# Second attention of a two-stage kernel: one ScalarE copy moved within its round, and the last batch's last four heads added by VectorE

## The chip, the cores and the metric

The kernel runs on one core of a Trainium2 chip. The metric is device time in microseconds of that core, as the median of several executions. A profiled execution gives instruction times of the core's engines: TensorE (PE; its weight loads are shown apart as PEld), VectorE (DVE), ScalarE (ACT), GpSimd (POOL) and SyncE (SP), which here only starts DMAs.

## The reference, cut to what matters

Two stages over x of shape (8, 512, 512). The first stage is a gated cross-attention whose result, x1, goes to DRAM; the change doesn't touch it. The second stage is this, for each of the 8 batches:

```python
# x: layernorm of x1; h = 8 heads, dh = 64, e = 5 experts, SEL = 2
q = (x @ Wq).reshape(b, t, h, dh).transpose(0, 2, 1, 3)
k = (x @ Wk).reshape(b, t, h, dh).transpose(0, 2, 1, 3)
gl_v = (x @ Ws).reshape(b, t, h, e)
wv = _topk_mask(gl_v, SEL) * jax.nn.sigmoid(gl_v)
xv = jnp.einsum('btd,edk->btek', x, Wv)
v = jnp.einsum('bthe,btek->bhtk', wv, xv)
scores = jnp.einsum('bhid,bhjd->bhij', q * scale, k)
probs = jax.nn.softmax(scores, axis=-1)
attn = jnp.einsum('bhij,bhjd->bihd', probs, v)
gl_o = (x @ Wd).reshape(b, t, h, e)
mask_o = _topk_mask(gl_o, SEL)
out = jnp.einsum('bthe,bthk,ekd->btd', mask_o, attn, Wo)
# result: x1 + tanh(g_ffn) * out
```

## The kernel before, in words

**Tiling.** A batch has 512 rows, which are 4 row tiles (t = 0 to 3) of 128. The 8 heads are taken in 4 pairs. Each head has 4 row tiles of scores, so a batch has 32 tiles of 128x512 scores (STEPS). Products of fp32 accuracy are made of three fp32r matmuls, of a high part, which ScalarE copies out of PSUM, and a low part, which VectorE forms as the difference.

**Rounds.** The order of the work is written out by hand. A round is four tiles of scores: it has the places SCORES, BEFORE, TURNS, BEHIND and AFTER, in this order on each engine. In SCORES, TensorE multiplies the scores, VectorE takes row maxima (L1496) and ScalarE the exponentials (L1370). In TURNS, TensorE transposes the four tiles of probabilities (L1791), and ScalarE copies the transposed tiles to SBUF as `pt` (probs_copy, L1379). The other units of work (`AT`) have a round and a place: turn_y is the transposition of the normalised x1, experts is the product with the stacked expert and gate weights (L1743), q and k are their products (L1734), values is probabilities times values (L1804), turn_o the transposition of a pair's output (L1749), turn_z and result the transposition of z and the product with Wo (L1757, L1767). Scores occupy rounds 0 to 7 of a batch; its units run from round -3 to round 12. So the steady loop (`Fori(0, B - 1)`, 7 passes) runs rounds 5 to 12 of batch b together with rounds -3 to 4 of batch b + 1. Rounds 5 to 12 of the last batch follow by themselves.

**Three shared banks.** All of these units but values write to one of three PSUM banks of `ps_r`, in turn, in the order `ORDER` of the steady loop. TensorE waits, before a unit, until the unit that is three places earlier in `ORDER` has been read (wait_bank, wait_read). In round 6 of batch b, which is round -2 of batch b + 1, the order on the banks is: experts 0, turn_y 2, turn_y 3 (place BEFORE), then experts 1, experts 2 (place BEHIND), then turn_o 1 (AFTER). So experts 1 uses the bank of experts 0 and waits for both of its copies, which are ScalarE's: `logits` (L1405) and `xv` (L1408). The copies of experts 0 begin with a wait for `v_steps`, GpSimd's count of steps, which says that the values of all pairs of the batch before are mixed and that `xv` may be overwritten.

```python
elif name == "experts":
    act.wait_ge(ex_ps, b * NT + n + 1)
    if n == 0 and not first:

        act.wait_ge(v_steps, b * PAIRS * V_STEPS)
        act.wait_ge(mask_ready, b)
```

**The mix over experts.** GpSimd mixes the values of each pair (mix_values: multiplications L1313, additions L1319). The output of the attention goes to z, 128 rows x 320 (5 experts x 64) per row tile, which is the sum over heads of (normalised output of the head) x (coefficient of row, head and expert). For each head h, VectorE makes a product over all four row tiles and experts, 128x1280 (mix_product, L1510; head 0 writes z, the others `z_tmp`, two buffers in turn). GpSimd adds heads 1 to 5 to z (mix_sums, L1331), and VectorE heads 6 and 7 (mix_sum, L1521). The products of pair p stand in rounds 5, 7, 9 and 10, and the coefficients in rounds 3, 5, 7 and 8 (L1534). Then ScalarE copies the last 64 columns of z once more (copy_last, L1423), z is transposed in three column tiles, ScalarE and VectorE split it (L1418, L1558), the four results are multiplied out, VectorE adds each to the residual (L1565), and SyncE stores it.

Of the kernel before, what the change touches and what calls it, by code (L numbers as in the profile page):

```python
# [20 lines left out]
F32 = mybir.dt.float32  # L21
# [3 lines left out]
ALU = mybir.AluOpType  # L25
# [3 lines left out]
P = 128  # L29
# [986 lines left out]
def expert_attention(nc, block, both, x1, g_ffn, wk, wo, out):  # L1016
# [3 lines left out]
    B, T, D = x1.shape  # L1020
# [58 lines left out]


    CUT = 5
    assert all(CUT - ROUNDS <= n < CUT + ROUNDS for n, place in AT.values())

    def units_at(n, *places):

        return [what for what, at in AT.items() if at[0] == n and at[1] in places]
# [9 lines left out]
    def bank_of(what):  # L1096
        return ORDER.index(what) % RING

    with ExitStack() as mem:
# [3 lines left out]
        def sem(name):  # L1103
            return mem.enter_context(nc.semaphore(name + "_2"))
# [83 lines left out]
        z_pool = sem("z_pool")  # L1188
        z_copied = sem("z_copied")
        z_ready = sem("z_ready")  # L1190
        zt_ps = sem("zt_ps")
# [98 lines left out]
        def _(pool):  # L1290
# [50 lines left out]
            with pool.Fori(0, B - 1) as b:  # L1341
                mix_sums(b, LAST_PAIR - 1)
                mix_values(b + 1, 0)
                rest(b + 1)
            mix_sums(B - 1, LAST_PAIR - 1)

        @block.scalar
        def _(act):
# [76 lines left out]
            def step(b, n, place, first=False):  # L1425
# [9 lines left out]
                elif place == BEFORE:  # L1435
                    if n == COPY_LAST_AT:
                        copy_last(b)
                    units_hi(b, units_at(n, BEFORE), first)
                    if n == 0:

                        act.wait_ge(logits_ready, b * NT + NT)
                        act.activation(sig[:], logits[:, 0], ACT.Exp, scale=-1.0).then_inc(sig_exp, 1)
                elif place == TURNS:
                    if 0 <= n < ROUNDS:
                        for tile in range(n * BANKS, n * BANKS + BANKS):
                            probs_copy(b, tile, first)
                elif place == BEHIND:
                    if n == NORMALISE_AT and not first:
                        normalise(b, (2, 3))
                    units_hi(b, units_at(n, BEHIND, AFTER), first)  # L1450

# [15 lines left out]
            with act.Fori(0, B - 1) as b:  # L1467
                for n in range(CUT, CUT + ROUNDS):
                    for place in PLACES:
                        step(b, n, place)  # L1470
                        step(b + 1, n - ROUNDS, place)
            for n in range(CUT, CUT + ROUNDS):
                for place in PLACES:
                    step(B - 1, n, place)

        @block.vector
        def _(dve):
# [170 lines left out]
            def units_lo(b, units, first):  # L1648
                for name, i in units:
                    if name != "values" and not (first and name == "turn_y"):  # L1650
                        part_lo(b, name, i)

            dve.wait_ge(both.feat_ps, B * NT)

# [10 lines left out]
            with dve.Fori(0, B - 1) as b:  # L1665
                for n in range(CUT, CUT + ROUNDS):
                    for place in PLACES:
                        step(b, n, place)
                        step(b + 1, n - ROUNDS, place)
            for n in range(CUT, CUT + ROUNDS):  # L1670
                for place in PLACES:
                    step(B - 1, n, place)

        @block.tensor
        def _(pe):
# [37 lines left out]
            def shared(b, name, n, first, last):  # L1713
# [45 lines left out]
                else:  # L1759
                    if n == 0:  # L1760
                        pe.wait_ge(w_lo["wo"], KZ)
                        pe.wait_ge(cleared, 2)
                    every = [(k, l, r) for k in range(LAST) for l, r in PASSES] + [(LAST, 1, 0), (LAST, 1, 1)]
                    for m, (k, l, r) in enumerate(every):
                        if n == 0 and m % len(PASSES) == 0:
                            pe.wait_ge(zt_lo, b * KZ + k + 1)
                        end = pe.matmul(ps, z_t2[:, l, k, n * P:(n + 1) * P], wo2[:, r, k, :],  # L1767
                                        start=m == 0, stop=m == len(every) - 1)
                    end.then_inc(res_ps, 1)

# [24 lines left out]
            def values(b, p, first):  # L1795
# [10 lines left out]
                end.then_inc(o_ps, 1)  # L1806

            def step(b, n, place, first=False, last=False):

# [13 lines left out]
            with pe.Fori(0, B - 1) as b:  # L1823
                for n in range(CUT, CUT + ROUNDS):
                    for place in PLACES:
                        step(b, n, place)
                        step(b + 1, n - ROUNDS, place)
            for n in range(CUT, CUT + ROUNDS):
                for place in PLACES:
                    step(B - 1, n, place, last=True)  # L1830


# [65 lines left out]
```

## Time and profile before

| | |
|---|---|
| Median of 3 runs | 1232.3 us (1231.46 to 1234.57) |
| Profiled execution, its own time | 1232.12 us |
| Its span in the profile | 1230.3 us |
| TensorE busy | 1187.6 us, 97% of the span |
| VectorE busy | 832.2 us, 68% |
| GpSimd busy | 662.3 us, 54% |
| ScalarE busy | 642.5 us, 52% |

The span is the time from the first to the last record of the profile; the time of the execution has 1.8 us more around it. Times in the rows are microseconds from the start of the span. One pass of the steady loop takes 86.6 us.

### The profile page before, as it was taken

The numbers are of one execution on the slowest core, as the hardware profiler recorded it, in microseconds if no ns is written. First come the engines' busy times: TensorE is split into PE (matmuls) and PEld (weight loads), VectorE is DVE, ScalarE is ACT, GpSimd is POOL, SyncE is SP. The second block draws the span as 40 slices with busy tenths as digits, with TensorE's granted clock in tenths as the row PEclk, the third lists the DMA queues.
The fourth block names the chain that finished last, engine by engine and source line by source line (L and its number), as shares of the span: only waits on it lengthen the run. The fifth ranks groups of instructions, "written<-read, shape, count | busy, mean of one in ns | idle before, by whom it ended". The sixth has DMA issues, their size and how long they took to land.

```text
span 1230.3 us, 19712 instructions
## 1 busy us (share of the span) xinstructions
PE 1187.6 (97%) x6344; PEld 912.0 (74%) x6344; DVE 832.2 (68%) x1526; ACT 642.5 (52%) x1431; POOL 662.3 (54%) x481
## 2 busy tenths in 40 slices
PE   5899999999999999999999999999999999999995
PEld 4678888888888887875767767777777777777663
DVE  6777777777777766367575674766765765756765
ACT  5443434334343433467566666566656666666661
POOL 1724242424242425339379297397496494692893
PEclk9899999999999999999999999999999999999998
DMA  6341414141414122410002002002011011020010
GB/s 206 119 129 43 128 43 128 43 128 43 128 43 128 43 94 99 153 50 1 35 2 90 13 0 102 0 20 83 0 43 59 0 68 34 0 68 0 0 69 35
DMA packets 40746, 75.87 MB, mean 62 GB/s; under 512 B 3728, under 2 KB 4240, under 8 KB 40720
## 3 DMA queue, kind: packets, MB, share of 16 engines
q1 hardware_dynamic: 40720, 75.55, 18.4%
q8 instruction: 13, 0.21, 0.1%
q14 instruction: 13, 0.11, 0.0%
HBM read 58.76 MB, written 16.78 MB: 61 GB/s over the span
## 4 chain that ended last, share of the span: by engine, by line
PE 66%; POOL 22%; DVE 5%; issue 5%; ACT 1%; POOLq 1%; DMA 0%; SPq 0%; DVEq 0%
PE ps_f L878 20%; POOL spare L1319 10%; POOL spare L1313 10%; PE ps_r L1734 8%; PE ps_h L878 8%; PE ps_s L878 7%; PE ps_r L1743 5%; PE ps_s L1791 4%; PE ps_s L1783 4%; PE ps_o L1804 4%; PE ps_r L1767 2%; PE ps_t L912 1%; DVE nmax L1496 1%; DVE z_tmp L1510 1%; POOL z L1331 1%
## 5 line engine op out<-in xcount | busy, mean ns | idle before, releaser
L1370 ACT ACTIVATE tmp<-ps_s,nmax 128x512 f32<-128x512 f32 x256 | 172.7, 688 | 106.8 <-DVE nmax L1496 106.8
L1496 DVE TENSOR_REDUCE nmax<-ps_s 128x1 f32<-128x512 f32 x256 | 158.7, 682 | 100.0 <-PE ps_s L1783 99.7
L1331 POOL TENSOR_TENSOR z<-z,z_tmp 128x1280 f32<-128x1280 f32 x40 | 117.1, 2928 | 178.8 <-DVE z_tmp L1510 176.1
L1313 POOL TENSOR_TENSOR spare<-xv,pick 128x512 f32<-128x512 f32 x160 | 168.1, 1051 | 34.8 <-DVE pick L1605 21.7
L1319 POOL TENSOR_TENSOR spare<-spare 128x512 f32<-128x512 f32 x128 | 180.5, 1410 | 10.0
L1379 ACT ACTIVATE pt<-ps_s 128x512 f32<-128x512 f32 x256 | 132.6, 621 | 10.8 <-PE ps_s L1791 10.8
L1791 PE MATMUL ps_s<-ident,tmp 128*128 128x128 f32 x1024 | 125.0, 273 | 2.6 <-ACT tmp L1370 2.5
L1791 PEld LDWEIGHTS ps_s<-ident,tmp 128*128 128x128 f32 x1024 | 114.9, 140 | 13.4 <-ACT tmp L1370 6.9
L1804 PE MATMUL ps_o<-pt,spare 128*64 128x512 f32 x512 | 116.9, 598 | 0.0
L255 POOL TENSOR_TENSOR e_t<-e_t 128x512 fp32r<-128x512 f32 x32 | 40.7, 1296 | 141.5 <-ACT e_t L474 141.5
L1783 PE MATMUL ps_s<-k,q 64*128 64x512 f32 x768 | 107.0, 409 | 2.2 <-DVE k L1552 1.5
L1783 PEld LDWEIGHTS ps_s<-k,q 64*128 64x128 f32 x768 | 67.4, 184 | 46.1 <-issue 34.0
L255 POOL TENSOR_TENSOR c<-stage,c 128x512 fp32r<-128x512 f32 x28 | 42.4, 1544 | 105.7 <-ACT c L251 105.7
L878 PE MATMUL ps_s<-c_t,es_t 128*128 128x512 f32 x384 | 96.2, 403 | 2.9 <-DVE es_t L255 2.9
L878 PE MATMUL ps_h<-es_t,c 128*128 128x512 f32 x384 | 98.8, 407 | 0.0
L1734 PE MATMUL ps_r<-es_t,wk 128*128 128x512 f32 x384 | 97.1, 401 | 0.0
L1734 PE MATMUL ps_r<-es_t,c_t 128*128 128x512 f32 x384 | 96.6, 400 | 0.0
L878 PE MATMUL ps_f<-weh,eh_t 128*128 128x512 f32 x384 | 94.7, 396 | 0.0
L878 PE MATMUL ps_f<-wh,h_t 128*128 128x512 f32 x384 | 93.5, 393 | 0.0
L878 PE MATMUL ps_f<-wec,e_t 128*128 128x512 f32 x384 | 92.3, 393 | 0.4 <-DVE wec L255 0.4
L878 PEld LDWEIGHTS ps_s<-c_t,es_t 128*128 128x128 f32 x384 | 72.4, 192 | 19.2 <-DVE es_t L255 4.1
L1734 PEld LDWEIGHTS ps_r<-es_t,wk 128*128 128x128 f32 x384 | 70.3, 188 | 21.0 <-issue 5.8
(183 smaller groups left out, 2100.1 us busy)
## 6 DMA issues: line engine op xcount, KB each, us to landing
stage<-in_x SPq DMA_DIRECT2D x32, 256.0 KB, 3.1
x_sb<-in_x SPq DMA_DIRECT2D x8, 1024.0 KB, 5.3
x_dram<-x_sb SPq DMA_DIRECT2D x32, 256.0 KB, 2.6
stage<-x_dram SPq DMA_DIRECT2D x8, 1024.0 KB, 5.7
x_sb<-x_dram SPq DMA_DIRECT2D x8, 1024.0 KB, 5.7
out_dram<-x_sb SPq DMA_DIRECT2D x32, 256.0 KB, 2.0
stage<-in_ctx_t SPq DMA_DIRECT2D x28, 256.0 KB, 2.8
stage<-in_ctx SPq DMA_DIRECT2D x28, 256.0 KB, 2.7
```

The costliest lines, as they stand in the source:

```text
L255: return eng.tensor_tensor(pair[:, 1, k, :], operand[:, k, :], pair[:, 0, k, :].bitcast(F32), ALU.subtract)
L878: last = pe.matmul(out, left(l, k), right(r, k), start=start and n == 1, stop=stop and n == ND * len(PASSES))
L1313: pool.tensor_tensor(v_tmp[:] if e else acc, xv[:, :, e, :].unsqueeze(2).broadcast_to(shape), pick[:, 0, e, :, 2 * p:2 * p + 2].unsqueeze( ...
L1319: pool.tensor_tensor(acc, acc, v_tmp[:], ALU.add).then_inc(v_steps, 1)
L1331: pool.tensor_tensor(zv, zv, z_tmp[:, h % 2], ALU.add).then_inc(z_pool, 1)
L1370: act.activation(probs[:, n % BANKS, :], ps_s[:, n % BANKS, :], ACT.Exp, bias=nmax[:, n:n + 1], accum_out=den[:, h, t:t + 1]).then_inc(p_e ...
L1379: act.activation(pt[:, h % 4, :, t * P:(t + 1) * P], ps_s[:, n % BANKS, :].rearrange("p (k t) -> p k t", k=NT), ACT.Copy).then_inc(pt_read ...
L1496: dve.tensor_reduce(nmax[:, n:n + 1], ps_s[:, n % BANKS, :], AX_X, ALU.max, negate=True).then_inc(nmax_ready, 1)
L1734: end = pe.matmul(ps, w2[:, l, k, n * P:(n + 1) * P], y_t2[:, r, k, :], start=m == 0, stop=m == len(every) - 1)
L1783: end = pe.matmul(ps_s[:, (n + a) % BANKS, :], q2[head_rows(a), p % 2, l, t * P:(t + 1) * P], k2[head_rows(a), p % 2, r, :], start=m == 0, ...
L1791: end = pe.transpose(ps_s[:, n % BANKS, k * P:(k + 1) * P], probs[:, n % BANKS, k * P:(k + 1) * P], ident[:])
L1804: end = pe.matmul(ps_o[head_rows(a), :], v_acc[:, p, k, a, :], pt[:, p % 2 * 2 + a, k, :], start=k == 0, stop=k == NT - 1)
```

## The change: what it does

First, the name LATE. The two ScalarE copies of the unit experts 0 leave the place BEFORE of round -2, where they stood ahead of the copies of turn_y 2 and turn_y 3 and ahead of the four copies of probabilities, and go to the place BEHIND of the same round, behind these six copies and ahead of the copies of experts 1. TensorE's order and its waits stay as they are. This concerns all 7 passes of the steady loop, and the prologue, where no probabilities are copied in that round.

Second, the last batch's end. Rounds 5 to 9 of it stay for TensorE and ScalarE, 5 to 8 for VectorE. GpSimd no longer adds heads 4 and 5 of the last batch. Heads 4 to 7 are added to z by VectorE, with one instruction for each head, row tile and expert (add_head): z's 128x64 share becomes coefficient x (128x64 of PSUM) + share. For heads 4 and 5 all four row tiles are done; for heads 6 and 7 and what follows, row tile by row tile: after the two heads of tile t its last 64 columns are copied again (copy_share), TensorE transposes the tile's three column tiles into one bank, ScalarE copies them in two pieces, VectorE forms the low part of the tile before (end_lo) and adds the result of the tile before that (end_out). TensorE makes 24 transpositions of the identity, whose output is not used, after turn_o 3.

```diff
--- before.py
+++ after.py
@@ -1078,6 +1078,12 @@
     COPY_LAST_AT = 11
+    LATE = ("experts", 0)
+    END_AT = 9
     CUT = 5
     assert all(CUT - ROUNDS <= n < CUT + ROUNDS for n, place in AT.values())
@@ -1095,6 +1101,8 @@
     def bank_of(what):
         return ORDER.index(what) % RING
+    END_BANKS = [bank for bank in range(RING) if bank != bank_of(("turn_o", PAIRS - 1))]
     with ExitStack() as mem:
         def sb(name, shape, dt=F32):
@@ -1187,6 +1195,7 @@
         z_dve = sem("z_dve")
         z_pool = sem("z_pool")
         z_copied = sem("z_copied")
+        z_heads = sem("z_heads")
         z_ready = sem("z_ready")
         zt_ps = sem("zt_ps")
         zt_hi = sem("zt_hi")
@@ -1342,7 +1351,6 @@
                 mix_sums(b, LAST_PAIR - 1)
                 mix_values(b + 1, 0)
                 rest(b + 1)
-            mix_sums(B - 1, LAST_PAIR - 1)
         @block.scalar
         def _(act):
@@ -1435,7 +1443,7 @@
                 elif place == BEFORE:
                     if n == COPY_LAST_AT:
                         copy_last(b)
-                    units_hi(b, units_at(n, BEFORE), first)
+                    units_hi(b, [what for what in units_at(n, BEFORE) if what != LATE], first)
                     if n == 0:
                         act.wait_ge(logits_ready, b * NT + NT)
@@ -1447,6 +1455,8 @@
                 elif place == BEHIND:
                     if n == NORMALISE_AT and not first:
                         normalise(b, (2, 3))
+                    if n == AT[LATE][0]:
+                        units_hi(b, [LATE], first)
                     units_hi(b, units_at(n, BEHIND, AFTER), first)
             def units_hi(b, units, first):
@@ -1469,9 +1479,15 @@
                     for place in PLACES:
                         step(b, n, place)
                         step(b + 1, n - ROUNDS, place)
-            for n in range(CUT, CUT + ROUNDS):
+            for n in range(CUT, END_AT + 1):
                 for place in PLACES:
                     step(B - 1, n, place)
+            out_copy(B - 1, LAST_PAIR, False)
+            for t in range(NT):
+                act.wait_ge(zt_ps, (B - 1) * KZ + t + 1)
+                turned = ps_r[:, END_BANKS[t % 2], 0:KZ * P].rearrange("p (k t) -> p k t", k=KZ)
+                act.activation(z_t2[:, 0, 0:LAST, t * P:(t + 1) * P], turned[:, 0:LAST, :], ACT.Copy)
+                act.activation(z_t2[:, 1, LAST, t * P:(t + 1) * P], turned[:, LAST, :], ACT.Copy).then_inc(zt_hi, 1)
         @block.vector
         def _(dve):
@@ -1650,6 +1666,58 @@
                     if name != "values" and not (first and name == "turn_y"):
                         part_lo(b, name, i)
+            def add_head(h, t, end=False):
+                ps = ps_r[:, bank_of(("turn_o", h // 2)), :].rearrange("p (t a k) -> p t a k", t=NT, a=2)[:, t, h % 2, :]
+                for e in range(E):
+                    share = z[:, t, e * DH:(e + 1) * DH]
+                    last = dve.scalar_tensor_tensor(share, ps, coef[:, h, t, e:e + 1], share, ALU.mult, ALU.add)
+                return last
+            def copy_share(t):
+                dve.tensor_scalar(z_all[:, t, NV:KZ * P], z[:, t, NV - HALF:NV], 1.0, None, ALU.mult).then_inc(z_ready, 1)
+            def end():
+                b = B - 1
+                first_sums = b * POOL_SUMS + 2 * LAST_PAIR - 3
+                dve.wait_ge(z_pool, first_sums)
+                dve.wait_ge(to_ps, b * PAIRS + LAST_PAIR)
+                for h in (2 * LAST_PAIR - 2, 2 * LAST_PAIR - 1):
+                    if h % 2:
+                        dve.wait_ge(z_heads, 1)
+                    for t in range(NT):
+                        last = add_head(h, t)
+                    last.then_inc(z_heads, 1)
+                dve.wait_ge(to_ps, b * PAIRS + PAIRS)
+                for t in range(NT + 2):
+                    if t < NT:
+                        dve.wait_ge(z_heads, 2 + 2 * t)
+                        add_head(2 * LAST_PAIR, t).then_inc(z_heads, 1)
+                        dve.wait_ge(z_heads, 3 + 2 * t)
+                        add_head(H - 1, t).then_inc(z_heads, 1)
+                        dve.wait_ge(z_heads, 4 + 2 * t)
+                        copy_share(t)
+                    if 1 <= t <= NT:
+                        end_lo(b, t - 1)
+                    if t >= 2:
+                        end_out(b, t - 2)
+            def end_lo(b, t):
+                cols = slice(t * P, (t + 1) * P)
+                turned = ps_r[:, END_BANKS[t % 2], 0:KZ * P].rearrange("p (k t) -> p k t", k=KZ)
+                dve.wait_ge(zt_hi, b * KZ + t + 1)
+                dve.tensor_tensor(z_t2[:, 1, 0:LAST, cols], turned[:, 0:LAST, :], z_t2[:, 0, 0:LAST, cols].bitcast(F32),
+                                  ALU.subtract)
+                dve.tensor_tensor(z_t2[HALF:P, 1, LAST, cols], turned[HALF:P, LAST, :],
+                                  z_t2[HALF:P, 1, LAST, cols].bitcast(F32), ALU.subtract).then_inc(zt_lo, 1)
+            def end_out(b, t):
+                if t == 0:
+                    dve.wait_ge(xres_loaded, b * 16 + 16)
+                dve.wait_ge(res_ps, b * NT + t + 1)
+                dve.scalar_tensor_tensor(x_res[:, t, :], ps_s[:, t, :], gate[:, 0:1], x_res[:, t, :],
+                                         ALU.mult, ALU.add).then_inc(out_ready, 1)
             dve.wait_ge(both.feat_ps, B * NT)
             dve.memset(norm[:], 0.0).then_inc(out_ready, NT)
@@ -1667,9 +1735,10 @@
                     for place in PLACES:
                         step(b, n, place)
                         step(b + 1, n - ROUNDS, place)
-            for n in range(CUT, CUT + ROUNDS):
+            for n in range(CUT, END_AT):
                 for place in PLACES:
                     step(B - 1, n, place)
+            end()
         @block.tensor
         def _(pe):
@@ -1760,13 +1829,16 @@
                     if n == 0:
                         pe.wait_ge(w_lo["wo"], KZ)
                         pe.wait_ge(cleared, 2)
-                    every = [(k, l, r) for k in range(LAST) for l, r in PASSES] + [(LAST, 1, 0), (LAST, 1, 1)]
-                    for m, (k, l, r) in enumerate(every):
-                        if n == 0 and m % len(PASSES) == 0:
-                            pe.wait_ge(zt_lo, b * KZ + k + 1)
-                        end = pe.matmul(ps, z_t2[:, l, k, n * P:(n + 1) * P], wo2[:, r, k, :],
-                                        start=m == 0, stop=m == len(every) - 1)
-                    end.then_inc(res_ps, 1)
+                    result(ps, n, (lambda k: pe.wait_ge(zt_lo, b * KZ + k + 1)) if n == 0 else None)
+            def result(ps, t, ready=None):
+                every = [(k, l, r) for k in range(LAST) for l, r in PASSES] + [(LAST, 1, 0), (LAST, 1, 1)]
+                for m, (k, l, r) in enumerate(every):
+                    if ready and m % len(PASSES) == 0:
+                        ready(k)
+                    last = pe.matmul(ps, z_t2[:, l, k, t * P:(t + 1) * P], wo2[:, r, k, :], start=m == 0,
+                                     stop=m == len(every) - 1)
+                last.then_inc(res_ps, 1)
             def scores(b, n, first):
@@ -1804,6 +1876,24 @@
                         end = pe.matmul(ps_o[head_rows(a), :], v_acc[:, p, k, a, :], pt[:, p % 2 * 2 + a, k, :],
                                         start=k == 0, stop=k == NT - 1)
                 end.then_inc(o_ps, 1)
+            def end(b):
+                shared(b, "turn_o", LAST_PAIR, False, True)
+                for _ in range(24):
+                    pe.transpose(ps_s[:, NT - 1, 0:P], ident[:], ident[:])
+                for t in range(NT + 1):
+                    if t < NT:
+                        pe.wait_ge(z_ready, b * 2 + t + 1)
+                        if t >= 2:
+                            pe.wait_ge(zt_lo, b * KZ + t - 1)
+                        for k in range(KZ):
+                            last = pe.transpose(ps_r[:, END_BANKS[t % 2], k * P:(k + 1) * P],
+                                                z_all[:, t, k * P:(k + 1) * P], ident[:])
+                        last.then_inc(zt_ps, 1)
+                    if t:
+                        pe.wait_ge(zt_lo, b * KZ + t)
+                        result(ps_s[:, t - 1, :], t - 1)
             def step(b, n, place, first=False, last=False):
@@ -1825,9 +1915,10 @@
                     for place in PLACES:
                         step(b, n, place)
                         step(b + 1, n - ROUNDS, place)
-            for n in range(CUT, CUT + ROUNDS):
+            for n in range(CUT, END_AT + 1):
                 for place in PLACES:
                     step(B - 1, n, place, last=True)
+            end(B - 1)
 def program(nc, x, ctx, ctx_t, g_xattn, g_ffn, w_sim, w_sim_cols, b_sim, w_qv, b_qv, wq, wk, w_vsd, wo, x1, out):
```

## Rows read from the trace of the kernel before

**Rows 1.** Page: busy time, share, instructions of each engine; slices of the granted clock.

```profile
PE 1187.6 (97%) x6344; PEld 912.0 (74%) x6344; DVE 832.2 (68%) x1526; ACT 642.5 (52%) x1431; POOL 662.3 (54%) x481
...
PEclk9899999999999999999999999999999999999998
```

**Rows 2.** Waits of TensorE, whole span: total, times, longest, in us.

```profile
PE ps_r L1757 <- DVE z L1521: 7.8, 1, 7.8
...
PE ps_r L1743 <- ACT logits L1405: 4.6, 8, 1.5
```

**Rows 3.** All waits from 540 to 1210 us, the same columns.

```profile
ACT logits L1405 <- POOL spare L1319: 13.4, 7, 2.0
```

**Rows 4.** Timeline, last steady pass, round 6: start, us, engine, line, operation, idle before.

```profile
1105.18 1.03 PE L1725 MATMUL ps_r<-ident,stage 128*128 128x128 f32 x8
...
1105.61 0.21 ACT L1370 ACTIVATION_READ_ACCUMULATOR tmp<-ps_s,nmax 128x1 f32 x1
...
1106.05 1.91 PE L1791 MATMUL ps_s<-ident,tmp 128*128 128x128 f32 x16
...
1106.41 1.27 POOL L1319 TENSOR_TENSOR spare<-spare 128x512 f32<-128x512 f32 x1
...
1107.71 0.24 ACT L1405 ACTIVATE logits<-ps_r 128x80 f32<-128x80 f32 x1 [1.89 <-POOL spare L1319]
1107.84 0.43 ACT L1408 ACTIVATE xv<-ps_r 128x320 f32<-128x320 f32 x1
...
1108.16 1.10 ACT L1397 ACTIVATE es_t<-ps_r 128x512 fp32r<-128x512 f32 x2
...
1108.37 4.57 PE L1743 MATMUL ps_r<-c,es_t 128*128 128x400 f32 x24 [0.41 <-ACT logits L1405]
...
1109.12 2.10 ACT L1379 ACTIVATE pt<-ps_s 128x512 f32<-128x512 f32 x4
```

**Rows 5.** Timeline, the last batch's end.

```profile
1197.67 5.88 POOL L1331 TENSOR_TENSOR z<-z,z_tmp 128x1280 f32<-128x1280 f32 x2 [0.35 <-DVE z_tmp L1510]
...
1203.53 2.88 DVE L1510 TENSOR_TENSOR z_tmp<-ps_r,coef 128x1280 f32<-128x1280 f32 x2
...
1205.09 5.92 POOL L1331 TENSOR_TENSOR z<-z,z_tmp 128x1280 f32<-128x1280 f32 x2 [1.54 <-DVE z_tmp L1510]
...
1207.22 0.63 PE L1749 MATMUL ps_r<-ident,spare 128*128 128x128 f32 x4 [0.79 <-ACT spare L1387]
...
1212.45 3.08 DVE L1521 TENSOR_TENSOR z<-z,z_tmp 128x1280 f32<-128x1280 f32 x2
...
1218.26 8.81 PE L1767 MATMUL ps_r<-wo,z_t 128*128 128x512 f32 x32
...
1227.11 0.75 DVE L1565 SCALAR_TENSOR_TENSOR x_sb<-ps_r,gate,x_sb 128x512 f32<-128x512 f32 x1 [1.10 <-PE ps_r L1767]
```

**Rows 6.** Timeline of VectorE, first stage.

```profile
130.27 0.23 DVE L645 TENSOR_SCALAR ew<-ew,bsim_col 128x4 f32<-128x4 f32 x1
130.41 1.00 DVE L631 TENSOR_SCALAR tmp<-e_t,w_cols 128x512 f32<-128x512 f32 x2
...
133.39 0.75 DVE L814 SCALAR_TENSOR_TENSOR x_sb<-ps_f,gate,x_sb 128x512 f32<-128x512 f32 x1
134.06 0.54 DVE L631 TENSOR_SCALAR tmp<-e_t,w_cols 128x512 f32<-128x512 f32 x1
```

**Rows 7.** Groups by line and form: busy us, mean ns of one, idle before.

```profile
L1548 DVE SCALAR_TENSOR_TENSOR q<-ps_r,q 128x512 fp32r<-128x512 f32 x32 | 21.8, 682 | 20.3 <-ACT q L1412 20.3
```

**Rows 8.** Busy time by stretch (engines in turn), granted clock (PEclk), DMA share, GB/s.

```profile
32.60:36.70 4.10, 0.66 (x4) 0.42 (x4) 2.83 (x14) 3.75 (x9) 1.24 (x2) 0.96 0.72 254
...
514.00:517.60 3.60, 2.10 (x12) 1.78 (x11) 1.46 (x3) 2.64 (x6) 2.55 (x3) 1.00 0.42 159
1210.52:1215.60 5.08, 0.00 (x0) 0.00 (x0) 4.38 (x3) 0.04 (x1) 0.48 (x1) 0.50 0.00 0
1215.60:1220.70 5.10, 5.03 (x18) 4.41 (x19) 2.08 (x3) 2.17 (x4) 0.00 (x0) 0.50 0.01 3
```


## The prediction

> **What bounds the kernel now.** I read the page first: TensorE is busy for 97% of the span, at the full clock (2.4 GHz) in nearly every slice [rows 1]. So an edit pays only if it removes TensorE work, which this one doesn't, or a wait of TensorE, and it costs wherever it adds one. Then the waits of TensorE: in the second attention only two matter. One is short and comes again: the product with the experts (L1743) waits for ScalarE's copies of experts 0, 8 times, 4.6 us in all, of which 1.5 us is in the first one. The other comes once: the transposition of z at the end of the last batch waits 7.8 us for VectorE [rows 2]. Then the stretch around each, in the timeline. Both parts of the change lie at one of these two waits.
>
> **The copies of experts 0, before.** In the last steady pass ScalarE is done with the exponentials of round 6 at 1105.61 + 0.21 = 1105.82. It then stands for 1.89 us in the wait for GpSimd's last mix step, which ends at 1106.41 + 1.27 = 1107.68. Then come `logits` at 1107.71, `xv` at 1107.84 to 1108.27, two copies for turn_y (1108.16), four of probabilities (1109.12). TensorE has finished its transpositions at 1106.05 + 1.91 = 1107.96, waits 0.41 us for `xv`, whose bank experts 1 needs, and goes on at 1108.37 [rows 4]. ScalarE's wait for GpSimd comes in all 7 passes, 13.4 us [rows 3]. It looks costly, but only 0.41 us of each reaches TensorE, because the transpositions run beside it.
>
> **The same, after.** ScalarE begins the two turn_y copies at about 1105.85: their transpositions (1105.18, eight in 1.03 us) come through in time. From the start of these two to the start of the first copy of probabilities it takes 1109.12 - 1108.16 = 0.96 us, so that one starts at 1106.81. Four of them take 2.10 us, 0.52 from start to start and the last 0.62 at most. Each also needs its own transposition: the last of them ends at 1107.96, and its copy isn't due before 1106.81 + 3 x 0.52 = 1108.37, so they don't hold it up. They end at 1108.9. GpSimd's step (1107.68) is by then long past; that wait is gone. `logits` starts at 1108.8 in place of 1107.71, `xv` ends at about 1109.35 in place of 1108.27, and experts 1 starts at about 1109.45 in place of 1108.37 [rows 4]. TensorE waits 1.45 us in place of 0.41: **+1.05 us a pass, +7.4 us in 7 passes**. Nothing gives it back: what has become earlier (turn_y and probabilities, by 2.3 us) is waited for by no TensorE instruction of this place, and the sum of all other waits of TensorE in the steady passes is too small to absorb it [rows 2]. Behind the stalled product on TensorE's queue stand experts 2, turn_o 1 and round 7, all the later by the same amount. In the prologue no probabilities are copied in that round, so it costs nothing there.
>
> Bounds: the last copy of probabilities can't begin before 1107.96, so if ScalarE is quicker in the other copies, `xv` ends at 1107.96 + 0.62 + 0.13 + 0.43 = 1109.14, 0.87 us later than before; take 0.7 with an overlap as between other copies. If the copies run end to end and each of the last ones waits for its transposition, it is 1.5. Seven passes: 4.9 to 10.5 us. A stall of this length doesn't cost the clock: before 517.6 TensorE was busy for 2.10 of 3.60 us and the clock stayed at 1.00; in 32.6 to 36.7 it was busy for 0.66 of 4.10, and the fall began [rows 8].
>
> **The end of the last batch, before.** GpSimd ends head 3 at 1197.67 + 5.88 = 1203.55. Then follow in a chain VectorE's products, GpSimd's heads 4 and 5 (to 1211.01), heads 6 and 7 on VectorE (to 1215.53), the transpositions, four results, and the last addition, which ends at 1227.11 + 0.75 = 1227.86: 24.3 us in all [rows 5].
>
> **The same, after.** Removed are two GpSimd additions (5.92 us), four products of 1.44 us and two sums (3.08 us). Added are 80 instructions of 128x64 with a coefficient from memory. No row shows one, so I work it out. With such a coefficient, the instruction of 128x512 takes 0.75 us, and the next one starts 0.67 us after it; the one of 128x4 takes 0.23 us, and the next starts 0.14 us after it [rows 6]. That is 1.04 ns an element, and for 64 elements 0.14 + 60 x 0.00104 = 0.20 us from start to start, and 0.28 us for one alone. Below: without a coefficient 128x512 takes 682 ns [rows 7], 0.07 us less, so 0.13. Above: 0.28, if they don't overlap. I take 0.20.
>
> Heads 4 and 5: 40 instructions, 8.0 us, from 1203.6 to 1211.6. Each row tile: 10 instructions and the copy, with waits of VectorE for itself, 2.3 us. Tile 0 is ready at 1213.9, tile 1 at 1216.3. Now each tile also brings the low part (128x256 and 64x128, 0.6 us) and the addition to the residual (0.66 us) of earlier tiles: tile 2 at 1219.2, tile 3 at 1222.8 if TensorE is never late. Then the transpositions (0.5), ScalarE's two copies (0.6) and the low part (0.6) give 1224.6. A result takes 8.81/4 = 2.2 us with part of them at half clock, 1.9 at full: result 2 ends at 1225.2, result 3 at 1227.1, the addition at 1227.9 [rows 5]. So with a full clock the end stands where it stood: 24.3 us by another way. GpSimd's 5.9 us come back as VectorE's.
>
> The clock: TensorE has 24 transpositions to do after 1207.9 (0.12 us each, to 1210.7), and then only 0.4 us until 1216.8. Before, with nothing to do from 1207.85, it ran at 0.50 (1.2 GHz) from 1210.52, and after 5.1 us of steady work it was back [rows 8]. So I expect the fall at about 1214 and the return at about 1222, since the slow results keep TensorE busy. Result 0 then ends at 1221.1 and holds VectorE up by 1.4 us: **+1.4 us**. If the clock stays low to the end, each of the last results is 3.7 us: +7. If the instructions take 0.13, with the clock returning as above: -1.6, with a full clock -5.1. If 0.28: +5.8.
>
> A page of the Trainium skill speaks of this spacing, "VectorE: DVE Perf Modes", section "The DRAIN you can't avoid": the next instruction doesn't start until the pipe of the one before is empty. By that rule the 80 would follow each other at their full length of 0.28 us and the end would be 5.8 us later than now in place of 1.4; rows 6, where the next one starts 0.09 us before the end, don't agree with it.
>
> **Sum.** The profiled execution's 1232.12 us (its span and 1.8 us) + 7.4 + 1.4 = 1240.9 us. It stands 0.2 us below the median of the runs; I predict 1241.
>
> **Rivals.** (a) The wait just goes. If experts 1 weren't held by the later copies, the 0.41 us of stall would go in 7 passes: -2.9, +1.4 for the end: 1230.6 us, not slower. For it speaks ScalarE's wait of 13.4 us [rows 3], against it that TensorE resumes 0.1 us behind the end of `xv` [rows 4]. It decides if ScalarE's copies hold TensorE by under 0.33 us more a pass: (3.7 - 1.4)/7.
> (b) The small instructions don't overlap (0.28 us): 1232.1 + 7.4 + 5.8 = 1245.3. For it: VectorE waits for itself between heads; against it, rows 6.
> (c) The small instructions are cheap (0.13): 1232.1 + 7.4 - 1.6 = 1237.9, with a full clock 1234.4.
> (d) The clock stays at half to the end: 1232.1 + 7.4 + 7 = 1246.5. For it: TensorE has gaps between the row tiles. Against it: at half clock its work fills them.
> (e) ScalarE is later by 1.5 us a pass: 1244.
>
> **How the numbers follow.** A difference of 0.3%, 3.7 us, is about what a measurement of this kernel can tell from no change. Chances: the forecast 0.57, (a) 0.09, (b) 0.09, (c) 0.12, (d) 0.07, (e) 0.06. The range from 1235 to 1246 takes in the bounds of the copies (4.9 with the end: 1238.4; 10.5: 1244) and (b), (c), (e), but leaves out (a) and (d). Slower by over 0.3%: 0.87, of which (c) with a full clock is the lower edge; within: 0.09; faster by more: 0.04, if (a) holds and the small instructions are cheap.
>
> **What would show it.** Right: in each pass TensorE waits about 1.45 us before the second of the experts' products, ScalarE no longer for GpSimd, and a pass takes 87.6 in place of 86.6 us; at the end 0.20 us from start to start of VectorE's additions, tile 0 ready 10.3 us behind GpSimd's last sum, the last addition about 24 to 26 us behind it. Wrong: a pass of 86.6 us or less, or the 80 instructions at another spacing, or a clock that doesn't return.

## The result, and the profile after

The changed kernel takes 1241.74 us (median, 1241.14 to 1242.46), against 1232.08 us before (median of four runs): ratio 1.0074, 95% interval 1.0062 to 1.0086. It is slower by 9.7 us. The profiled execution took 1241.14 us, with a span of 1239.4.

TensorE's waits in the whole span, in the columns of [rows 2]:

```profile
PE ps_r L1812 <- ACT logits L1413: 11.7, 8, 1.5
...
PE ps_r L1891 <- DVE z L1678: 5.7, 3, 3.6
```

The wait for the copies of experts 0 has grown from 4.6 to 11.7 us over the same 8 times: the first is still 1.5 us, the 7 of the loop are 1.46 in place of 0.44 each. The wait at the end was one of 7.8 us. Now there are three, 5.7 us in all and the longest 3.6: TensorE waits for one row tile at a time, and 24 transpositions of the identity (2.78 us) fill a part of the gap.

Round 6 of the last steady pass in the timeline after, against [rows 4]:

```profile
1112.16 0.21 ACT L1378 ACTIVATION_READ_ACCUMULATOR tmp<-ps_s,nmax 128x1 f32 x1
1112.37 1.08 ACT L1405 ACTIVATE es_t<-ps_r 128x512 fp32r<-128x512 f32 x2
...
1112.60 1.91 PE L1863 MATMUL ps_s<-ident,tmp 128*128 128x128 f32 x16
...
1113.34 2.08 ACT L1387 ACTIVATE pt<-ps_s 128x512 f32<-128x512 f32 x4
...
1115.24 0.30 ACT L1413 ACTIVATE logits<-ps_r 128x80 f32<-128x80 f32 x1
1115.36 0.51 ACT L1416 ACTIVATE xv<-ps_r 128x320 f32<-128x320 f32 x1
...
1115.97 4.57 PE L1812 MATMUL ps_r<-c,es_t 128*128 128x400 f32 x24 [1.46 <-ACT logits L1413]
```

ScalarE doesn't stand any more: 1112.37 follows directly on the last record of its exponentials. But `logits` comes behind six copies (two for turn_y, four of probabilities), 2.64 us after the start of TensorE's transpositions (1112.60) in place of 1.66 us, and TensorE's next product starts 3.37 us after it in place of 2.32: 1.05 us later. The length of the seven passes is read between two marks, the start of GpSimd's first addition to z of the first batch and of the last. Before:

```profile
588.11 2.94 POOL L1331 TENSOR_TENSOR z<-z,z_tmp 128x1280 f32<-128x1280 f32 x1
...
1194.41 2.90 POOL L1331 TENSOR_TENSOR z<-z,z_tmp 128x1280 f32<-128x1280 f32 x1 [0.17 <-POOL spare L1319]
```

And after:

```profile
588.55 2.90 POOL L1340 TENSOR_TENSOR z<-z,z_tmp 128x1280 f32<-128x1280 f32 x1
...
1201.95 2.90 POOL L1340 TENSOR_TENSOR z<-z,z_tmp 128x1280 f32<-128x1280 f32 x1 [0.17 <-POOL spare L1328]
```

That is 613.40 us in place of 606.30: 7.10 us for 7 passes. In the four experiments below whose passes are those of the kernel before (2, 7, 8 and 9) the same stretch takes 605.93 to 606.27 us, so it repeats within 0.4 us.

The end of the last batch, timeline after, against [rows 5]:

```profile
1205.24 5.89 POOL L1340 TENSOR_TENSOR z<-z,z_tmp 128x1280 f32<-128x1280 f32 x2 [0.39 <-DVE z_tmp L1526]
...
1211.17 10.13 DVE L1674 SCALAR_TENSOR_TENSOR z<-ps_r,coef,z 128x64 f32<-128x64 f32 x50
...
1221.33 0.20 DVE L1678 TENSOR_SCALAR z<-z 128x64 f32<-128x64 f32 x1
...
1221.58 0.55 PE L1891 MATMUL ps_r<-ident,z 128*128 128x128 f32 x3 [3.55 <-DVE z L1678]
...
1223.61 0.20 DVE L1678 TENSOR_SCALAR z<-z 128x64 f32<-128x64 f32 x1
...
1224.49 3.78 PE L1839 MATMUL ps_s<-wo,z_t 128*128 128x512 f32 x8
...
1228.38 0.75 DVE L1718 SCALAR_TENSOR_TENSOR x_sb<-ps_s,gate,x_sb 128x512 f32<-128x512 f32 x1 [0.91 <-PE ps_s L1839]
...
1232.10 3.99 PE L1839 MATMUL ps_s<-wo,z_t 128*128 128x512 f32 x16
...
1236.13 0.75 DVE L1718 SCALAR_TENSOR_TENSOR x_sb<-ps_s,gate,x_sb 128x512 f32<-128x512 f32 x1 [1.11 <-PE ps_s L1839]
```

VectorE starts on heads 4 and 5 when GpSimd is done, at 1211.13. 50 small additions take 10.13 us, 0.203 each. Row tile 0 is ready at 1221.5; its result takes TensorE 3.78 us, and VectorE waits 0.91 us for it. The last addition ends at 1236.88, 25.75 us behind GpSimd; before it was 24.31.

TensorE's clock there, by stretches of 2 us (columns as in [rows 8]):

```profile
1220.00:1222.00 2.00, 0.42 (x3) 0.31 (x3) 1.93 (x11) 0.00 (x0) 0.00 (x0) 1.00 0.02 4
1222.00:1224.00 2.00, 0.27 (x3) 0.15 (x2) 1.93 (x10) 0.55 (x2) 0.00 (x0) 0.62 0.00 0
1224.00:1226.00 2.00, 2.00 (x7) 1.58 (x8) 1.92 (x10) 0.55 (x2) 0.00 (x0) 0.50 0.00 0
...
1228.00:1230.00 2.00, 2.00 (x9) 1.70 (x8) 1.62 (x6) 0.55 (x2) 0.00 (x0) 0.67 0.01 4
1230.00:1232.00 2.00, 1.55 (x8) 0.81 (x6) 1.92 (x9) 0.00 (x0) 0.00 (x0) 1.00 0.34 127
```

After the 24 transpositions TensorE had nothing to do for 3.55 us. By the means of these stretches the clock fell from 2.4 to 1.2 GHz at about 1222.5 and came back at about 1229.3.

The three parts, from the profiles: 7.10 us in the passes, 25.75 - 24.31 = 1.44 us at the end, and 0.48 us by which the second attention begins later (not the change's doing, see the end), 9.02 of the 9.1 us between the spans. The 9.7 us between the medians has 0.6 more: the median of the changed kernel lies that far above its profiled execution, and no stage can be named for it.

### The profile page after: what moved, and what is told of

Its sections match the earlier page's. It is cut to its first block, busy times and chain, and to the rows that moved or that the text cites. A ratio compares the mean times of both kernels' runs of the same rounds, so it can differ in the third digit from the quotient of the medians.

```text
span 1239.4 us, 19839 instructions
## 1 busy us (share of the span) xinstructions
PE 1191.2 (96%) x6368; PEld 915.3 (74%) x6368; DVE 841.3 (68%) x1609; ACT 643.0 (52%) x1435; POOL 655.9 (53%) x479
## 4 chain that ended last, share of the span: by engine, by line
PE 89%; DVE 5%; ACT 4%; issue 2%; POOL 0%; DMA 0%; SPq 0%; ACTq 0%; POOLq 0%; DVEq 0%
PE ps_f L878 20%; PE ps_r L1803 15%; PE ps_o L1876 9%; PE ps_s L1863 8%; PE ps_s L1855 8%; PE ps_h L878 8%; PE ps_s L878 7%; PE ps_r L1812 4%; PE ps_r L1839 4%; ACT tmp L1378 1%; ACT pt L1387 1%; PE ps_r L1818 1%; PE ps_t L912 1%; DVE z L1674 1%; PE ps_r L1826 1%
## 5 line engine op out<-in xcount | busy, mean ns | idle before, releaser
L1340 POOL TENSOR_TENSOR z<-z,z_tmp 128x1280 f32<-128x1280 f32 x38 | 111.0, 2922 | 184.8 <-DVE z_tmp L1526 182.3
L1863 PEld LDWEIGHTS ps_s<-ident,tmp 128*128 128x128 f32 x1024 | 114.9, 141 | 13.4 <-ACT tmp L1378 7.0
L1812 PE MATMUL ps_r<-c,es_t 128*128 128x400 f32 x384 | 75.6, 348 | 11.7 <-ACT logits L1413 11.7
```

The source lines that it names most:

```text
L1340: pool.tensor_tensor(zv, zv, z_tmp[:, h % 2], ALU.add).then_inc(z_pool, 1)
L1812: end = pe.matmul(ps[:, 0:NX], y_t2[:, l, k, n * P:(n + 1) * P], wx2[:, r, k, :], start=m == 0, stop=m == len(every) - 1)
L1863: end = pe.transpose(ps_s[:, n % BANKS, k * P:(k + 1) * P], probs[:, n % BANKS, k * P:(k + 1) * P], ident[:])
```

## The experiments

Each ratio is to the kernel before, measured beside the experiment (medians 1232.39, 1232.57 and 1232.35 us). "The seven passes" are the stretch between the two marks above, and "the end" is the time from the end of GpSimd's addition of head 3 of the last batch (its last one where the end is new) to the end of VectorE's last addition.

**1. The first part alone** (`late_only`): before, with LATE.

```diff
+    LATE = ("experts", 0)
...
-                    units_hi(b, units_at(n, BEFORE), first)
+                    units_hi(b, [what for what in units_at(n, BEFORE) if what != LATE], first)
...
+                    if n == AT[LATE][0]:
+                        units_hi(b, [LATE], first)
                     units_hi(b, units_at(n, BEHIND, AFTER), first)
```

> The kernel before with the first part of the change alone: the copies of experts 0 stand behind the probabilities' copies. My theory: TensorE waits about 1.45 us in place of 0.41 in each of the 7 passes, +7.4 us, so 1239.6 us where the kernel before takes 1232.1; the end of the last batch takes 24.3 us as before. The rival theory, that most of the 9.7 us comes from VectorE's small additions at the end: 1234 us or less.

Measured: 1240.76 us against 1232.39, ratio 1.0064 (1.0051 to 1.0078). TensorE's wait for the copies is 11.7 us, as in the changed kernel; from the first pass's addition (589.90) to the last batch's (1203.21) it is 613.31 us. The loss in the passes is this part's. The other 1.4 us of the 8.4 between the medians isn't the passes': in this profile the second attention begins 1.8 us later than in that of the kernel before, and the end takes 24.55 us.

**2. The end alone** (`end_only`): the changed kernel without LATE in ScalarE's steps.

```diff
-                    units_hi(b, [what for what in units_at(n, BEFORE) if what != LATE], first)
+                    units_hi(b, units_at(n, BEFORE), first)
...
-                    if n == AT[LATE][0]:
-                        units_hi(b, [LATE], first)
```

> The changed kernel with the copies of experts 0 back at their place before: only the end of the last batch is new. My theory: +1.4 us, 1233.6 us, and a pass of 86.6 us. The rival theory, that the small additions carry most of the loss: 1238 us or more.

Measured: 1234.21 us, ratio 1.0014 (1.0005 to 1.0023). The seven passes take 606.21 us. Two rows of its timeline: GpSimd's last sum, and VectorE's last addition.

```profile
1197.75 5.88 POOL L1340 TENSOR_TENSOR z<-z,z_tmp 128x1280 f32<-128x1280 f32 x2 [0.35 <-DVE z_tmp L1524]
...
1228.63 0.75 DVE L1716 SCALAR_TENSOR_TENSOR x_sb<-ps_s,gate,x_sb 128x512 f32<-128x512 f32 x1 [1.12 <-PE ps_s L1837]
```

From 1203.63 to 1229.38 it is 25.75 us, the same as in the changed kernel.

**3. Behind turn_y, ahead of the probabilities** (`late_turns`): the kernel before, with this edit.

```diff
-                    units_hi(b, units_at(n, BEFORE), first)
+                    units_hi(b, sorted(units_at(n, BEFORE), key=lambda what: what == ("experts", 0)), first)
```

> The kernel before, with the copies of experts 0 behind those of turn_y 2 and 3, but still ahead of the probabilities' copies. If it is the four probabilities' copies (2.1 us) that hold TensorE, as I think, the two turn_y copies fit into ScalarE's wait for GpSimd (1.9 us), experts 0 is copied when it was before, and the time is that of the kernel before, 1232.1 us within 1 us, with TensorE's wait at 0.4 us. If any later place in ScalarE's queue costs (the rival), the wait grows by the two copies, about 1.0 us a pass: 1239 us.

Measured: 1232.30 us, ratio 0.9997 (0.9988 to 1.0006). The seven passes take 605.85 us. The two copies lie inside ScalarE's wait, which shrinks from 1.89 to 0.78 us:

```profile
1107.45 1.09 ACT L1397 ACTIVATE es_t<-ps_r 128x512 fp32r<-128x512 f32 x2
...
1109.32 0.24 ACT L1405 ACTIVATE logits<-ps_r 128x80 f32<-128x80 f32 x1 [0.78 <-POOL spare L1319]
```

**4. Half a dose** (`late_two`): two of the probabilities' copies ahead of those of experts 0.

```diff
-                    units_hi(b, units_at(n, BEFORE), first)
+                    units_hi(b, [what for what in units_at(n, BEFORE) if first or what != LATE], first)
...
                         for tile in range(n * BANKS, n * BANKS + BANKS):
+                            if tile == n * BANKS + 2 and more and n == AT[LATE][0] + ROUNDS:
+                                units_hi(b + 1, [LATE], False)
                             probs_copy(b, tile, first)
```

> A half dose: the kernel before with the copies of experts 0 behind those of turn_y and behind two of the four probabilities' copies (0.52 us each), the other two behind them. My theory, that ScalarE's queue sets the start of experts 1 by what stands ahead: the copies start at about 1107.9 in place of 1107.7 and, with all four ahead, 1108.8, so +0.15 us a pass, +1 us: 1233.4 us. The rival, that any probabilities' copy ahead of them costs in full: half of the 7 us, 1236 us.

Measured: 1232.94 us, ratio 1.0002 (0.9993 to 1.0011). TensorE's wait:

```profile
PE ps_r L1747 <- ACT logits L1407: 4.9, 8, 1.5
```

4.9 us in place of 4.6, and the seven passes take 606.44 us, 0.14 more than before and within the scatter: I expected 1 us. So two of these copies cost next to nothing and four cost 7 us. What counts is when the queue reaches experts 0, against GpSimd's end.

**5. Experts 0 waits for the last multiplication** (`xv_early`): the kernel before, with this edit. The addition that is no longer waited for doesn't read `xv`.

```diff
-                        act.wait_ge(v_steps, b * PAIRS * V_STEPS)
+                        act.wait_ge(v_steps, b * PAIRS * V_STEPS - 1)
```

> The kernel before, but the copies of experts 0 wait for GpSimd's last multiplication of the batch before (the last step that reads xv) in place of the addition behind it, which takes 1.3 us. My theory: the copies start at about 1106.4 in place of 1107.7, xv is ready before TensorE has ended its transpositions, its 0.41 us of waiting goes in 7 passes: -2.9 us, 1229.2 us. The rival theory, that another wait takes its place at once (the bank of turn_y 2, or the low part that VectorE makes of it): no change.

Measured: 1227.13 us, ratio 0.9957 (0.9943 to 0.9970): 5.3 us faster, where I expected 2.9. The last steady pass:

```profile
1102.44 1.91 PE L1791 MATMUL ps_s<-ident,tmp 128*128 128x128 f32 x16
1102.74 0.24 ACT L1405 ACTIVATE logits<-ps_r 128x80 f32<-128x80 f32 x1 [0.52 <-POOL spare L1313]
...
1102.87 0.43 ACT L1408 ACTIVATE xv<-ps_r 128x320 f32<-128x320 f32 x1
...
1104.11 4.59 PE L1743 MATMUL ps_r<-c,es_t 128*128 128x400 f32 x24
```

ScalarE waits 0.52 us, and experts 1 starts 1.67 us after the start of the transpositions, before their shown end at 1104.35. It was 2.32 us before. So a pass of the kernel before lost 0.65 us there, and not only the 0.41 us shown as idle. The seven passes take 601.50 us (588.65 to 1190.15) in place of 606.30, 4.8 us less; the end, 23.46 us in place of 24.31, had the clock back sooner: by the means of stretches of 1 us the clock fell 8.4 us behind GpSimd's addition of head 3 and was back at 15.2, in place of 7.0 and 17.2.

**6. LATE with the earlier wait** (`late_xv`): experiment 1 with the edit of 5.

> The first part of the change, with experts 0 waiting for GpSimd's last multiplication as in the early-wait run. If the wait for GpSimd is long over when the copies' turn comes, as I hold, no change against the first part alone (1240.8 us): the order alone holds TensorE. If GpSimd still took part: 5 us less.

Measured: 1239.07 us, ratio 1.0049 (1.0035 to 1.0063). The median is 1.7 us below that of experiment 1. In the profiles 1.2 us lie ahead of the passes: the first product of the second attention starts at 514.38 in the one and at 515.61 in the other; the rest has no cause shown. But the passes aren't shorter: 588.76 to 1202.13, 613.37 us, and TensorE's wait is 11.7 us. Round 6 again:

```profile
1112.69 1.91 PE L1795 MATMUL ps_s<-ident,tmp 128*128 128x128 f32 x16
...
1115.34 0.29 ACT L1407 ACTIVATE logits<-ps_r 128x80 f32<-128x80 f32 x1
...
1116.06 4.57 PE L1747 MATMUL ps_r<-c,es_t 128*128 128x400 f32 x24 [1.46 <-ACT logits L1407]
```

3.37 us from the transpositions to the product, as in the changed kernel. GpSimd takes no part in the loss.

**7. A constant for the coefficient** (`end_const`): experiment 2 with this edit; heads 4 to 7 of the last batch are added without their coefficients.

```diff
-                    last = dve.scalar_tensor_tensor(share, ps, coef[:, h, t, e:e + 1], share, ALU.mult, ALU.add)
+                    last = dve.scalar_tensor_tensor(share, ps, 1.0, share, ALU.mult, ALU.add)
```

> The end alone, as in the run before, with the number 1.0 in place of the coefficient in VectorE's 80 small additions, so that the last batch's heads 4 to 7 are added unweighted. It measures what a coefficient read from memory costs in 80 instructions in a row: from start to start 0.13 us in place of 0.20 if it costs what the two forms of 128x512 show; heads 4 and 5 then take 5.4 us in place of 8.0, and the end about 3 us less, as TensorE then becomes late (1231.2 us). If the coefficient is hidden in such a row of instructions: 0.20 us and no change.

Measured: 1228.9 us, ratio 0.9971 (0.9961 to 0.9980), 5.3 us under experiment 2.

```profile
1203.77 7.09 DVE L1672 SCALAR_TENSOR_TENSOR z<-ps_r,z 128x64 f32<-128x64 f32 x50
...
1210.90 0.19 DVE L1676 TENSOR_SCALAR z<-z 128x64 f32<-128x64 f32 x1
...
1223.00 0.75 DVE L1716 SCALAR_TENSOR_TENSOR x_sb<-ps_s,gate,x_sb 128x512 f32<-128x512 f32 x1 [1.11 <-PE ps_s L1837]
```

The 50 additions take 7.09 us in place of 10.13: 0.142 each, so the coefficient costs 0.06 us an instruction. The end takes 20.01 us in place of 25.75, 5.7 saved where I expected 3: row tile 0 was ready at 1211.1, just behind the 24 transpositions, and the clock stayed at 1.00 to the last result. The saving is about what the parts give: 80 x 0.061 = 4.9 us for the coefficients (an estimate) and 0.9 us for the clock, which experiment 8 prices.

**8. TensorE kept busy** (`end_warm`): experiment 2 with 50 and 12 transpositions of the identity.

```diff
-                for _ in range(24):
+                for _ in range(50):
                     pe.transpose(ps_s[:, NT - 1, 0:P], ident[:], ident[:])
...
                         last.then_inc(zt_ps, 1)
+                        if t == 0:
+                            for _ in range(12):
+                                pe.transpose(ps_s[:, NT - 1, 0:P], ident[:], ident[:])
```

> The end alone, with 50 in place of 24 transpositions of the identity ahead of row tile 0 and 12 more behind its transpositions, so that TensorE isn't idle and its clock doesn't fall. My theory: the granted clock stays at 1.00 to the last result, result 0 ends within 2 us in place of 3.8, and the end of the batch takes 24.3 us in place of 25.7: -1.4 us. The rival, that VectorE alone sets the end: no change.

Measured: 1233.74 us, ratio 1.0007 (0.9997 to 1.0017). The granted clock is 1.00 to the end. From 1204.94 to the end of the last addition, 1229.81, it is 24.87 us: 0.88 us less than in experiment 2, where I expected 1.4. The last part of it:

```profile
1224.15 0.19 DVE L1676 TENSOR_SCALAR z<-z 128x64 f32<-128x64 f32 x1
...
1225.03 3.99 PE L1837 MATMUL ps_s<-wo,z_t 128*128 128x512 f32 x16
...
1229.06 0.75 DVE L1716 SCALAR_TENSOR_TENSOR x_sb<-ps_s,gate,x_sb 128x512 f32<-128x512 f32 x1 [1.11 <-PE ps_s L1837]
```

VectorE has no wait left but those for the last two results. Up to row tile 3, ready at 1224.34, the time is VectorE's own, 19.40 us; the 5.47 us behind it are TensorE's last two results (3.99 us), which begin 0.69 us later, and the last addition. The difference between the medians, 0.5 us, can't be told from none.

**9. Heads 4 and 5 in large pieces** (`end_prod`): experiment 2 with this edit.

```diff
-                for h in (2 * LAST_PAIR - 2, 2 * LAST_PAIR - 1):
-                    if h % 2:
-                        dve.wait_ge(z_heads, 1)
-                    for t in range(NT):
-                        last = add_head(h, t)
-                    last.then_inc(z_heads, 1)
+                for h in (2 * LAST_PAIR - 2, 2 * LAST_PAIR - 1):
+                    mix_product(b, h)
+                for h in (2 * LAST_PAIR - 2, 2 * LAST_PAIR - 1):
+                    dve.wait_ge(z_dve, b * H + h + 1)
+                    if h % 2:
+                        dve.wait_ge(z_heads, 1)
+                    zv = z.rearrange("p t (e k) -> p t e k", e=E)
+                    dve.tensor_tensor(zv, zv, z_tmp[:, h % 2], ALU.add).then_inc(z_heads, 1)
```

> The end alone, but heads 4 and 5 as VectorE's products of 128x1280 and sums of 128x1280 (two of each) in place of 40 small additions; heads 6 and 7 stay row tile by row tile. Two products take 2.9 us and two sums 3.1 us, 6.0 in all in place of 8.1: -2.1 us against the end alone. If TensorE's half clock is what sets the end (the rival), less than 1 us.

Measured: 1231.15 us, ratio 0.9991 (0.9981 to 1.0000), 3.1 us under experiment 2.

```profile
1203.48 2.89 DVE L1524 TENSOR_TENSOR z_tmp<-ps_r,coef 128x1280 f32<-128x1280 f32 x2
...
1206.28 3.07 DVE L1690 TENSOR_TENSOR z<-z,z_tmp 128x1280 f32<-128x1280 f32 x2
...
1209.46 2.14 DVE L1672 SCALAR_TENSOR_TENSOR z<-ps_r,coef,z 128x64 f32<-128x64 f32 x10
...
1225.93 0.75 DVE L1718 SCALAR_TENSOR_TENSOR x_sb<-ps_s,gate,x_sb 128x512 f32<-128x512 f32 x1 [1.11 <-PE ps_s L1839]
```

Four large instructions take 5.9 us, 40 small ones 40 x 0.203 = 8.1. Of these 8.1 us, 40 x 0.061 = 2.4 are the coefficients by experiment 7 (an estimate); without them the 40 would be about level with the four. The end is 23.23 us, 2.5 less, and 1.1 less than before the change.

**10. All that paid** (`best`): experiment 9, the wait of 5, and 32 and 12 transpositions of the identity.

> All that paid: the kernel before with experts 0 waiting for the last multiplication only (-5.2 us as measured), and the new end with heads 4 and 5 as products and sums (-2.1 against the end alone) and TensorE kept busy by 32 + 12 transpositions (-1.4). Sum: 1232.4 - 5.2 + 1.6 - 2.1 - 1.4 = 1225.3 us; if the end is bound elsewhere, 1227 as for the early wait alone.

Measured: 1225.94 us, ratio 0.9950 (0.9936 to 0.9964): 6.6 us faster than the kernel before, 15.8 faster than the changed one. GpSimd's last sum and VectorE's last addition:

```profile
1192.48 5.90 POOL L1340 TENSOR_TENSOR z<-z,z_tmp 128x1280 f32<-128x1280 f32 x2 [0.33 <-DVE z_tmp L1524]
...
1220.49 0.75 DVE L1718 SCALAR_TENSOR_TENSOR x_sb<-ps_s,gate,x_sb 128x512 f32<-128x512 f32 x1 [1.11 <-PE ps_s L1839]
```

The end takes 22.86 us. Against experiment 5 it gains 1.2 us, within what the two intervals leave open.

## Why the prediction was right

Predicted were 1241 us (1235 to 1246) and slower; measured are 1241.7. The terms add up to 8.8 us, and the passes and the end measured 8.5; another 1.1 us of the 9.7, 0.5 ahead of the passes and 0.6 between profile and median, stood in no term.

- **The copies of experts 0.** The step "ScalarE's queue reaches experts 0 at 1108.8 in place of 1107.71" holds: `logits` came 0.98 us later against the transpositions (1.09 predicted), TensorE's product 1.05 later (1.05 to 1.08), its wait was 1.46 us (1.45), and the passes took 7.1 us more (7.4). Experiments 1 and 2 give the loss to this part, 3 and 4 show that the two turn_y copies and two more cost next to nothing, because they lie inside the wait for GpSimd, and 6 that this wait no longer matters when all four are ahead. Rival (e), 1.5 us a pass, falls with the 1.05.
- **ScalarE's wait of 13.4 us** looked like the cost and wasn't. It cost TensorE only what was left of it behind the transpositions. The edit removed ScalarE's idle time and put six copies in its place, 2.87 us from the start of the first to `logits` (1112.37 to 1115.24), in front of the one copy that TensorE waits for. Rival (a), that the wait just goes, falls by this.
- **What the stall cost before** was the number that I had too small. I took the 0.41 us that the row shows as idle; experiment 5 shows 0.65. The difference between two placements was not touched by that, but the price of rival (a) was: without any stall it would have been faster by 4.6 us in the loop (7 x 0.65; experiment 5 has 4.8), not 2.9.
- **The clock in the passes** stayed at 1.00 with the longer stall (the mean from 540 to 1190 us), as the stretch before 517.6 had suggested [rows 8].
- **The small additions.** 0.20 us from start to start was predicted, 0.203 measured; row tile 0 was ready 10.4 us behind GpSimd (10.3); the end took 1.44 us more (1.4). Rivals (b) and (c) fall by this row. Some of the exactness is luck: the two rows under the estimate are of different operations, a SCALAR_TENSOR_TENSOR of 128x512 and a TENSOR_SCALAR of 128x4 [rows 6], and nothing said that one line would join them. Experiment 7 measures the coefficient by itself, 0.06 us (0.07 from the rows).
- **The clock at the end.** A fall at about 10.4 us and a return at about 18.4 us behind GpSimd's sum were predicted; they came at 11.4 and 18.2. Experiment 8 gives its price: 0.9 us, where my sum had 1.4. Two errors cancelled here. With a full clock the end takes 24.87 us and not 24.3: row tile 3 is ready 19.40 us behind GpSimd's last sum (19.25 in my sum), and what follows takes 5.47 us (5.1): TensorE's last two results start 0.69 us behind it and take 3.99 us, where I had 0.5 and 3.8. And the slow result held VectorE up by 0.91 us in place of 1.4. Rival (d) didn't come: TensorE was busy throughout from 1224.00 to 1230.00, and the clock was back after 6.8 us.

The sentence of the Trainium skill that was weighed above ("VectorE: DVE Perf Modes", "The DRAIN you can't avoid") doesn't describe this row of instructions: the next one starts 0.203 us after the one before, while each is 277 ns long. The prediction took the section's first rule without its exception: the section goes on: "A next op that is not held starts earlier". This trace agrees with that.

```profile
L1674 DVE SCALAR_TENSOR_TENSOR z<-ps_r,coef,z 128x64 f32<-128x64 f32 x80 | 16.2, 277 | 0.3
```

Another section of that page of the Trainium skill, "The TRN2 errata — SBUF-src ops pay a fixed extra latency per instruction", says that many small tiles pay a fixed cost each where a large one pays it once. Experiment 9 agrees in direction, with 8.1 us for 40 pieces against 5.9 us for the same additions in four instructions; no run here separates that cost from the others of a small piece, and 2.4 us of the 8.1 are the coefficients, by the estimate there.

## What to carry to other kernels

An engine's idle time in front of a wait isn't a cost of that wait, as long as the engine that sets the end has work beside it: follow the wait to the bound engine, and count what a moved step now stands behind. Where a buffer is released late, look first for the last instruction that reads it; here the release was one addition too late, and that was worth more than any order tried. When a serial chain is cut into pieces, price each piece from start to start, and count what the bound engine's clock does in the new gaps.

## What the runs showed that I had not expected

- The stall of TensorE ahead of experts 1 is longer than the idle time shown. Experts 1 can start 1.67 us after the start of the 16 transpositions, whose shown length is 1.91 us; with 0.41 us shown as idle the start was 0.65 us later than that. Start-to-start times tell what such a stall costs.
- The stage ahead of the change isn't equally long in all executions. The first product of the second attention (L1743) starts between 513.26 and 515.79 us in the twelve profiles, though the code ahead of it is the same. The granted clock of the first 60 us goes with it for the most part: its mean is 0.94 in seven of them, which start at 513.26 to 514.31, and 0.91 in the other five, at 514.25 to 515.79. Differences under 2 us between spans can't be read without taking this out; the stretch between two marks inside the stage can.
- The end isn't equally long either where its code is the same. In the six profiles with the old end it takes 24.31 us (the kernel before), 24.36 (experiment 4), 24.55 (1), 24.77 (6), 24.78 (3) and 23.46 (5). By the means of stretches of 1 us the clock falls 7.0 to 8.4 us behind GpSimd's addition in them and comes back at 15.2 to 18.2. The new end took 25.75 us both times. So the 1.44 us of the change's second part can't be told more closely than to about half a microsecond, and no run shows that the edit of experiment 5 made its end shorter.
